# GpSimd issues the three gathers of a chunk only when those of the chunk before have landed

## What is computed

```python
pos = base[None, :, None] + s_idx[None, None, :] * freq_avg[:, :, None] + phase_avg[:, :, None]
pos = jnp.clip(pos, 0.0, Ll - 1.0)
lo = jnp.floor(pos).astype(jnp.int32)
hi = jnp.minimum(lo + 1, Ll - 1)
g_lo = xh[b_ix, lo]
g_hi = xh[b_ix, hi]
g = g_lo + frac[..., None, None] * (g_hi - g_lo)
out_h = jnp.einsum('blshd,blhs->blhd', g, w)
```

## Time and profile before

| | |
|---|---|
| median of 3 runs | 2349.13 us (2343.15 to 2356.42) |
| profiled execution, span | 2353.6 us |
| PE busy | 1720.4 us, 73% |
| DVE busy | 1254.1 us, 53% |
| ACT busy | 988.0 us, 42% |
| POOL busy | 1103.7 us, 47% |
| mean granted TensorE clock | 0.854 of full speed |

### The profile page before, as it was taken

How to read it: one execution, slowest core, us unless ns; L and a number is a source line. 1 busy time by engine, 2 the same in 40 slices (tenths; PEclk the granted TensorE clock), 3 DMA queues, 4 the chain that set the end, 5 groups by cost and what they waited for, 6 DMA issues and landing times.

```text
span 2353.6 us, 31786 instructions
## 1 busy us (share of the span) xinstructions
PE 1720.4 (73%) x12145; PEld 1141.7 (49%) x12153; DVE 1254.1 (53%) x2158; ACT 988.0 (42%) x2363; POOL 1103.7 (47%) x1069
## 2 busy tenths in 40 slices
PE   5787876767777766666776766667787768879866
PEld 3354534445445534344555434454455346656645
DVE  6565645555556444555565545655565454343345
ACT  3365673234543551243353540335354533343333
POOL 0000016475556345664556255554665367766630
PEclk8799998778989877988898978789888879989876
DMA  3010023132223232232223232232233343223321
GB/s 133 10 24 14 19 48 96 58 102 83 79 75 103 63 74 79 79 96 73 88 79 90 56 95 70 83 90 72 86 89 85 69 148 99 88 81 90 88 47 36
DMA packets 93420, 178.72 MB, mean 76 GB/s; under 512 B 21452, under 2 KB 50264, under 8 KB 93016
## 3 DMA queue, kind: packets, MB, share of 16 engines
q0 software_dynamic: 50688, 138.48, 21.4%
q1 hardware_dynamic: 42584, 38.23, 5.8%
HBM read 151.46 MB, written 9.44 MB: 68 GB/s over the span
## 4 chain that ended last, share of the span: by engine, by line
PE 39%; DVE 19%; another core or an unknown queue 18%; ACT 12%; issue 9%; SPq 1%; POOL 1%; DMA 1%; DVEq 0%; POOLq 0%; ACTq 0%
PE c L1612 5%; DVE pool_c L1235 4%; PE pa L1508 3%; PE pb L1508 3%; PE ta L1542 2%; DVE ssq L1132 2%; PE ta L1516 2%; ACT pool_a L771 2%; ACT pool_a L836 2%; PE sc L1587 2%; DVE pool_a L1155 1%; DVE pool_a L1185 1%; PE tb L1389 1%; PE pb L1560 1%
## 5 line engine op out<-in xcount | busy, mean ns | idle before, releaser
L729 POOL DMA_INDIRECT pool_c<-rows_of_x,idx x1056 | 1100.9, 1043 | 1156.5 <-PE c L1612 380.0
L1612 PE MATMUL c<-ident,pool_c 128*128 128x128 f32 x2112 | 337.1, 303 | 61.6 <-DVE pool_c L1235 32.2
L1612 PEld LDWEIGHTS c<-ident,pool_c 128*128 128x128 f32 x2112 | 278.3, 158 | 143.0 <-issue 97.0
L1235 DVE TENSOR_TENSOR pool_c<-pool_c 128x768 f32<-128x768 f32 x352 | 331.3, 951 | 20.1 <-DMA pool_c<-rows_of_x,idx 19.7
L860 ACT ACTIVATE prob<-sc,nmax 128x128 f32<-128x128 f32 x512 | 179.3, 374 | 0.1
L1516 PE MATMUL ta<-ident,pool_a 128*128 128x128 f32 x512 | 90.9, 333 | 90.8 <-DVE pool_a L1155 80.4
L771 ACT COPY pool_a<-tb 128x512 f32<-128x512 f32 x188 | 112.5, 599 | 103.6 <-remote 58.3
L1155 DVE TENSOR_TENSOR pool_a<-ta,rinv 128x512 f32<-128x512 f32 x64 | 44.3, 692 | 199.9 <-remote 158.3
L1542 PE MATMUL ta<-vmix,pool_a 128*64 128x64 f32 x1024 | 80.9, 239 | 81.0 <-ACT pool_a L771 67.5
L1142 DVE TENSOR_REDUCE nmax<-sc 128x8 f32<-128x1024 f32 x64 | 77.5, 1211 | 103.9 <-remote 96.1
L1508 PE MATMUL pa<-wqkv,pool_a 128*128 128x512 f32 x192 | 118.8, 706 | 12.9 <-DVE pool_a L1185 7.4
(11 more groups left out here) (413 smaller groups left out, 3344.3 us busy)
## 6 DMA issues: line engine op xcount, KB each, us to landing
pool_c<-rows_of_x,idx POOLq DMA_INDIRECT x1056
vmix<-vring SPq DMA_DIRECT2D x128, 128.0 KB
rows_of_x<-x2tok SPq DMA_DIRECT2D x16, 256.0 KB
xtok<-in_x SPq DMA_DIRECT2D x4, 512.0 KB
x_of_all<-x2tok SPq DMA_DIRECT2D x8, 256.0 KB
out<-pool_c SPq DMA_DIRECT2D x8, 256.0 KB, 2.3
wqkv<-in_wqkv SPq DMA_DIRECT2D x1, 1536.0 KB
xtok<-x_of_all SPq DMA_DIRECT2D x3, 512.0 KB
```

Source lines behind the costliest of these rows:

```text
L729: pool.indirect_dma_start(gat[:, n % GB, s, :], None, tables[b % 2], bass.IndirectOffsetOnAxis(ap=idx[:, t, SC * c + s:SC * c + s + 1], ax ...
L1235: V.tensor_tensor(g4, g4, wv, ALU.mult).then_inc(SEM["c_prod"], 1)
L1612: ins = mm(out[:, c:c + P], x, ident[:], start=(i == 0 and k == 0), stop=(i == BCH - 1 and k == len(parts) - 1), is_transpose=True, skip_g ...
```

## The change

Before each chunk but the first of the first batch, POOL now also waits for the full count of the semaphore of the chunk before, which is the last chunk of the batch before where n is 0.

```diff
@@ def gather(b, n):
                 if n >= GB:
                     chunk_added(pool, b, n - GB)
                 else:
                     chunk_added(pool, b - 1, CHUNKS - 1 - (CHUNKS - 1 - n) % GB)
+                prev, of = (n - 1, b) if n else (CHUNKS - 1, b - 1)
+                if of >= 0:
+                    wait(pool, f"c_gather{prev % GB}", of, 16 * SC * (prev // GB + 1))
                 t, c = divmod(n, NCH)
                 for s in range(SC):
                     pool.indirect_dma_start(
```

## The result

| | median us | runs | against before, 95% interval |
|---|---|---|---|
| before | 2346.14 | 4 (2339.13 to 2356.42) | |
| changed | 2697.19 | 4 (2696.11 to 2700.61) | 1.1475 [1.1435, 1.1515] |

The change makes the kernel 14.7% slower. The forecast was 2700 us, in the range 2530 to 2800.

The account below looks back on a forecast made before the run. Gathers on POOL were to bound all four batches at 6.37 us per chunk (issue 3.73, landing 1.9, waking 0.74). The batches' +72.3, +60.8, +61.5 and +157.1 sum to +351.7 us: 2700 us by the median, range 2530 to 2800.

Parts of the forecast that it names:

- The gathers' pace binds all four batches: Likeliest case, chance 0.70: gathers become the bound in every batch, +351.7 us in all, giving 2700 us.
- The pace: Shortest time P from one chunk's first gather to the next one's: 3.73 + 1.9 + 0.74 = 6.37 us.
- Issue: On POOL, three gathers of 1.04 us with 0.30 us between two of them: 3.73 us per chunk.
- Landing: From a chunk's third gather's end until its data has landed: 1.9 us, 1.8 for most, one in twenty some 2 later.
- Waking: POOL's restart after the landing: 0.74 us for a wait in its own instruction; 0.28 us, carried by the gather, as low end.
- POOL wakes quickly: Rival, chance 0.14: POOL answers the new wait after 0.28 us, P is 5.91 us, 162 us less: 2539 us.
- The 2.30 us for a gather from end to end: Estimate for one 128 KB gather by a documentation page; with it P would be 5.72 us and the time 2472 us.
- Faster, by shorter holds: Rival, chance 0.03: in middle batches, shorter gather bursts release waiting engines sooner; faster only below P = 5.37 us, say 2289 us.

Follow-up runs that it names:

- e1_swap: The changed kernel with its two waits in the other order, so that the gather itself carries the wait for the landing: 2665.19 us, 1.1353 against before.
- e3: The changed kernel with the new wait only before even chunks, in all batches: 2335.26 us, 0.9955 against before.
- e6: The changed kernel with the new wait only before even chunks of the first three batches: 2293.43 us, 0.9806 against before.
- e8: As e6, but with the wait for the landing carried by the gather: 2271.08 us, 0.9722 against before.
- e11: As e8, but with the wait before every third chunk instead of every second, in the first three batches: 2305.53 us, 0.9807 against before.
- e7_pause: The kernel before with 24 empty instructions on POOL ahead of each chunk's gathers and no wait for a landing: 2349.69 us, 1.0019.
- e2_two_back: The changed kernel with POOL waiting for the chunk two before, so two chunks may be in flight: 2336.74 us, 0.9953 against before.

## Why the prediction was right

Point by point, by its own terms:

- **The gathers' pace binds all four batches: right.** The stretches grew by 70.5, 59.3, 61.4 and 156.8 us; forecast 72.3, 60.8, 61.5 and 157.1. Outside them the span changed by -0.7 us before the first gather and -2.7 us behind the last product, where the forecast had 0. The sum of all is +344.6 us; forecast +351.7.
- **The pace.** From the stretches, (571.3 - 12.3 + 0.7)/88 = 6.36 us, forecast 6.37. In the last batch it is (559.5 + 0.7)/88 = 6.37 us at a granted clock of 0.77 instead of 0.82, so the lower clock cost nothing there. The 12.3 us run from the last product to the next batch's first gather (1467.41 to 1479.69); I had 13.0, also for the third, where before really had 15 us; it made no difference, since all three are 12.3 us now.
- **Issue.** 3 x 1.011 + 0.60 = 3.63 us; I had 3.73. A little less, because the product of a chunk now starts ahead of the next chunk's first gather, and only that one meets it: the three gathers of a chunk take 1.09, 0.98 and 0.96 us on average, before 1.03, 1.06 and 1.04.
- **Landing.** POOL's 330 waits for a landing took 885.6 us, 2.68 us each. Less the waking, that is 2.68 - 0.71 = 1.97 us, forecast 1.9. The bet that the seven late waits of before were not the mean was right; so was the level of 1.8, which the common landing has (1.83), and so were the few late ones: 18 of the 330 waits are longer than 3.5 us. It stays a bet, for it took a mean from seven selected rows, and only 0.2 us more would have cost 70 us.
- **Waking.** 0.71 to 0.74 us. Which of the two rows applied was the largest open choice, worth 162 us by its own sum, and it was settled by the form of the instruction. That reasoning gave the right number. It wasn't right as a price: e1_swap changed the form, got the early waking, and kept only 32 of the 169 us, because the gather that starts sooner meets the product that the same landing has started. "POOL wakes quickly" would thus have given some 2665, not 2539 us. That the first gather would meet the product is the step which the prediction left out of this rival.
- **The 2.30 us for a gather from end to end**, the estimate by the Trainium skill's page "DMA: Bandwidth & Descriptors". The trace after has 0.94 + 1.80 = 2.74 us for one, and 2.9 us as the mean. The measurement decides: 2472 us would have been too low.
- **Faster, by shorter holds: right that they give nothing at this pace.** As a mechanism it isn't proved: with the wait put in thinly (e3, e6, e8, e11) the middle batches came out up to 34 us shorter than before, and a part of that goes with a higher clock. The rival had little weight because at one wait per chunk it can't show, and that held.

The mechanism was right, and that the number came out within 3 us (7 us for the profiled execution) is in part luck: the errors have opposite signs. Per chunk, issue was forecast 0.10 us too long (35 us in all) and waking up to 0.03, the landing 0.07 us too short (25 us).

**What stays open** is what the holds are. Shown is that ACT waits for results of PE that were ready 11 us earlier while gathers are issued back to back, that before has no wait on "remote" ahead of the first gather or behind the last product, and that these waits add up to less where POOL waits for a landing before every second chunk or every chunk. Whether they hang on gathers in flight, on the descriptors that wait in a queue, or on POOL's own activity was not told apart: e7_pause, meant for it, made no pause, and e2_two_back hardly changed the gathers. That a thin wait is faster is measured; that it gains by shorter holds is likely from the table and not proved.

## What to carry to other kernels

A wait for a landing costs, per use, the whole round trip (here 2.0 us of landing and 0.7 us of waking) times its number, if the issuing engine is close to the pace of its users; compare issue plus round trip with the users' time per chunk, stage by stage, and the sum comes out. The stage with the least time per chunk pays most: here 157 of 345 us fell on one batch of four. The same wait, put in before every second chunk and only where there is room for it, made this kernel 2.8% faster (e8_second_middle_swap, 1.7 to 3.9%), for a reason that is only partly known, so a throttle and its place should be tried apart from each other.

## What the runs showed of the hardware that I had not expected

- An indirect DMA issued while DVE multiplies two SBUF operands (0.96 us) took 1.54 us instead of 0.95, and ended 0.82 us behind that product, whether it began 0.24 or 0.71 us after the product's start. With a product of 0.24 us it took 0.95 us, and so it did under DVE work with at most one SBUF operand.
- 24 empty instructions written ahead of each chunk on POOL added nothing to the 0.30 us between two gathers. About one per chunk shows in the trace; what became of the others it doesn't show.
- POOL starts a gather 0.28 us behind the end of a sum when the gather itself carries the wait, and some 0.75 us behind it when an instruction of its own does.
- In stretches of gathers without a pause, ACT went on 11.2 us after PE had finished what it waited for; the longest wait put down to "remote" is 15.3 us. See above for what is shown of it, and that the cause is open.
